# Where the head's values are split, and how they are fetched, in a two-term fp32 attention kernel

## The chip, the core and the metric

The kernel runs on one core of one Trainium2 chip. The metric is device time in microseconds of one execution, from start to end of the program, and less is better. Five engines work side by side, each through its own list of instructions in order: TensorE (PE: matmuls, with its weight loads shown as PEld), VectorE (DVE), ScalarE (ACT), GpSimd (POOL) and SyncE (SP), which here issues every DMA. They meet only at semaphores: an engine that waits holds up everything that is behind the wait in its own list.

## What is computed

One transformer layer on x of 2048 x 256, in fp32: attention with 16 heads of width 128, and a gated feed-forward part. Cut to what matters here:

```python
xn = layernorm(x)
k, q, v = (einsum('ihd,bpd->biph', W, xn) for W in (W_K, W_Q, W_V))   # 16 heads of 128
scores = einsum('biph,biqh->biqp', k, q)
masked = scores * mask - 1e10 * (1 - mask)                            # causal
attn   = softmax(masked / sqrt(128))
z      = einsum('biqp,biph->biqh', attn, v)
out    = x + einsum('df,bqf->bqd', W_O, z_flat) + ffn(xn)
```

fp32 accuracy comes from two terms: each operand is split into a part `hi` (rounded to fp32r by ACT) and a part `lo` (the rest, subtracted by DVE or POOL), and each product is three matmuls, hi·hi, hi·lo and lo·hi (`mm3`, L970 to L972).

## The kernel before

A front part (the first 250 us or so) does the layer norm, the feed-forward part and the values of all heads, which go to DRAM as `all_values`, one block of 1 MB for each head. Then come 16 heads, one after the other, in 8 steps each (`period(h)`, written once for each engine; heads 1 to 14 are a hardware loop), and a short `over` period that ends the last head.

**A step.** Step s handles two rows of 128 queries: the big row 15 - s and the small row s, 17 tiles of 128 keys together. PE makes their scores into five PSUM banks (`scores`), DVE takes the row maxima (`maxima`, L887 to L895), ACT the exponentials into the SBUF buffer `raw` (`exponential`, L655, in three pieces), and DVE transposes 32x32 blocks in place (`transpose_blocks`, L902). The rest of the transposition is done by DMA through DRAM: SP sends the row to `scratch` (`send`, L353, eight DMAs a step: four for the big row, four for the small) and brings it back into `pt_lo` (`bring`, L367, two a step). Then ACT makes `pt_hi` (`p_to_hi`, L662), POOL makes `pt_lo` (`p_to_lo`, L462), both in three pieces, and PE multiplies with the values (`weighted_sum`).

**The order of SP.** In step s: bring of step s - 1, then send of step s. A bring waits until the sends of its row have landed; the send behind it in the list waits for `blocked` (the DVE transposes of step s). `raw` holds two steps, so ACT's first exponential of step s + 2 waits until the sends of step s have landed (`stored`).

**The weighted sums.** Eight chunks z of 256 queries a head, in the order 7, 0, 6, 1, 5, 2, 4, 3 (`Z_ORDER`). Those with even z (big, `Z_BIG`) are spread over two steps, those with odd z (`Z_SMALL`) take one. Chunk z = 0 of head h is multiplied in steps 4 (keys 8 to 15, values quarters 2 and 3) and 5 (keys 0 to 7, quarters 0 and 1). Each z is split again (`z_to_hi` on ACT, L673, `z_to_lo` on DVE, L906), multiplied with W_O on PE (`output`), scaled by ACT into `share` (L682) and added by POOL (`add`, L453).

**The values of a head.** `bring_v(h)` (L372) fetches 1 MB into `v_next` in one DMA, at the end of SP's step 5 of the head before, ahead of the bring of step 5. They are split in quarters of 512 columns: `v_to_hi` on ACT (L635) and `v_to_lo` on POOL (L467), quarter 3 in step 0, quarter 2 in step 3, and quarters 0 and 1 in step 4 (`V_AT`). In step 4 ACT does them behind the exponentials, `output` and `wo_to_hi`; POOL behind `add`. `v_to_hi(h, 0)` also waits for `z_product` of z = 7 of the head before (step 3 of PE).

**Keys and queries of the next head.** Made in slices by PE in steps 0 to 7 (`project_kq`), split by ACT (`kq_to_hi`, L596) and DVE (`kq_to_lo`, L866, L869). Slice K2 is PE's last work of step 7; in ACT's list it stands behind the three `p_to_hi` of step 7, and right behind it, at the start of step 0, stands `z_to_hi` of z = 3. On DVE `z_to_lo` of z = 3 stands ahead of the maxima of step 0.

Of the kernel before, what the change touches and what calls it, by code (L numbers as in the profile page):

```python
# [12 lines left out]
BANK = 512  # L13
# [5 lines left out]
def attention_ffn_kernel(nc, x, w_heads, w_values, w1t, w3t, w2t, hadamard, out):  # L19
# [11 lines left out]
    HEADS = w_heads.shape[0]  # L31
# [3 lines left out]
    QUARTERS = S // BANK  # L35
    PER_Q = BANK // P
# [53 lines left out]

    V_ITEMS = [3, 2, 0, 1]
    V_AT = {0: [3], 3: [2], 4: [0, 1]}
    KQ_FIRST = 6

    with ExitStack() as ctx:
# [3 lines left out]
        def sem(name):  # L99
            return ctx.enter_context(nc.semaphore(name))  # L100
# [140 lines left out]
        qk_split, wo_split = sem("qk_split"), sem("wo_split")  # L241
        projected, proj_hi, proj_lo = sem("projected"), sem("proj_hi"), sem("proj_lo")
        v_projected, v_copied, v_stored = sem("v_projected"), sem("v_copied"), [sem("v_stored0"), sem("v_stored1")]
        v_moved = sem("v_moved")
        late_projected, late_copied = sem("late_projected"), sem("late_copied")
        late_stored = [sem(f"late_stored{i}") for i in range(4)]
        v_hi_done, v_lo_done, v2_read = sem("v_hi_done"), sem("v_lo_done"), sem("v2_read")
# [19 lines left out]
        def wait(engine, semaphore, count):  # L267

            if not isinstance(count, int) or count > 0:
                engine.wait_ge(semaphore, count)  # L270
# [5 lines left out]
        def v_count(h, b):  # L276
            return QUARTERS * h + V_ITEMS.index(b) + 1
# [30 lines left out]
        def _(sp):  # L308
# [57 lines left out]
                to = pt_row(pt_lo, j).bitcast(F32).rearrange("p a i q -> p a (i q)")  # L366
                sp.dma_start(to, scratch[j].rearrange("p (a x) -> p a x", a=4)).then_inc(moved[small], 16)  # L367

            def bring_v(h):

                wait(sp, v_lo_done, QUARTERS * h)
                sp.dma_start(v_next[:, :], all_values[h].rearrange("p i d -> p (i d)")).then_inc(v_moved, 16)  # L372

            for i in range(2):
                sp.wait_ge(v_stored[i], 16 * TILES // 2)
            bring_v(0)
            for h in range(HEADS):
                for s in range(STEPS):
                    if s == 0 and h + 1 < HEADS:
                        sp.wait_ge(qk_split, h + 1)  # L380
                        sp.dma_start(w_raw[:, 0:2, :], w_heads[h + 1][:, 0:2, :]).then_inc(qk_loaded, 16)
                    if s == 6 and h + 1 < HEADS:
                        sp.wait_ge(wo_split, h + 1)
                        sp.dma_start(w_raw[:, 3, :], w_heads[h + 1][:, 2, :]).then_inc(wo_loaded, 16)
                    hh, ss = step_before(h, s, 1)
                    if hh >= 0 and not on_tensor(hh, ss):
                        bring(hh, ss, 0)
                        bring(hh, ss, 1)
                    if not on_tensor(h, s):
                        send(h, s, 0)  # L390
                        send(h, s, 1)
                    if h == 0 and s < 4:
                        store_late(2 * s)
                        store_late(2 * s + 1)
                    if h == 0 and s == 5:
                        for i in range(4):
                            sp.wait_ge(late_stored[i], 16 * LATE_UNITS // 4)
                    if s == 5 and h + 1 < HEADS:
                        bring_v(h + 1)
            for z in range(CHUNKS):  # L400
                c = Z_ORDER[z]
                sp.wait_ge(out_added, z_count(HEADS - 1, z))
# [4 lines left out]
        def _(pool):  # L407
# [62 lines left out]
            def period(h, first=False, more=True, over=False):  # L470

                for s in range(5 if over else STEPS):
                    if (s - 1) in O_BIG or s == 0:
                        back, z = O_BIG[(s - 1) % STEPS]
                        if s == 0:
                            back -= 1
                        if not (first and back) and not (over and not back):
                            add(h + back, z)
                    if s == 2 and more and not over:
                        split_qk(h + 1)  # L480
                    for b in [] if over else V_AT.get(s, []):
                        v_to_lo(h, b)
                    if s == 4 and not over:
                        split_o(h)
                    hh, ss = step_before(h, s, 2)
                    if not (first and s < 2) and not over:
                        for n in range(3):
                            p_to_lo(hh, ss, n)

                    if s != 2 and s in O_SMALL or s == 3:  # L490
                        back, z = O_SMALL[2 if s == 3 else s]
                        if not (first and back) and not (over and not back):
                            add(h + back, z)
# [21 lines left out]
        def _(act):  # L515
# [76 lines left out]
            def kq_to_hi(h, item):  # L592
                which, b = item
                to = (k_hi if which == "K" else q_hi)[:, b * BANK:(b + 1) * BANK]
                act.wait_ge(projected, kq_count(h, item))
                act.activation(to, kq_bank(h, item), ACT.Copy, scale=1.0 if which == "K" else SCALE  # L596
                               ).then_inc(proj_hi, 1)
# [26 lines left out]

            def v_to_hi(h, b):
                sl = slice(b * BANK, (b + 1) * BANK)
                act.wait_ge(v_moved, 16 * h + 16)

                if b == 3:
                    wait(act, z_product, z_count(h - 1, 2))  # L630
                elif b == 2:
                    wait(act, v2_read, h)
                elif b == 0:
                    wait(act, z_product, z_count(h - 1, 7))
                act.copy(v_hi[:, sl], v_next[:, sl]).then_inc(v_hi_done, 1)  # L635
# [50 lines left out]
            def period(h, first=False, more=True, over=False):  # L686
                def absent(back):
                    return first and back or over and not back

                for s in range(5 if over else STEPS):  # L690
                    if s == 0 and not absent(O_SMALL[s][0]):
                        z_to_hi(h + O_SMALL[s][0], O_SMALL[s][1])
                    if (s - 1) in O_BIG or s == 0:
                        back, z = O_BIG[(s - 1) % STEPS]
# [1 line left out]
                            back -= 1  # L696
                        if not absent(back):
                            output(h + back, z)
                    if s == 3 and not over:
                        v_to_hi(h, 2)  # L700
                    if s in (1, 3) and not absent(O_BIG[s][0]):
                        z_to_hi(h + O_BIG[s][0], O_BIG[s][1])
                    if not over:
# [20 lines left out]
                    if s == 3 and more and not over:  # L724
                        kq_to_hi(h, ("K", 3))
                    if s >= 5 and more and not over:
                        kq_to_hi(h, (("Q", 3), ("Q", 0), ("K", 1))[s - 5])
                    for b in [] if over or s == 3 else V_AT.get(s, []):
                        v_to_hi(h, b)
                    if first and s < 4:  # L730
                        late_copy(2 * s)
                        late_copy(2 * s + 1)
# [1 line left out]
                    if over and s < 2:  # L734
                        for n in range(5):
                            transposed_to_hi(5 * s + n)
                    if not (first and s < 2) and not over:
                        p_to_hi(hh, ss, 0)
                    if s in (1, 3, 5) and not absent(Z_SMALL[s][0]):
                        z_to_hi(h + Z_SMALL[s][0], Z_SMALL[s][1])  # L740
                    if not (first and s < 2) and not over:
                        p_to_hi(hh, ss, 1)
                        p_to_hi(hh, ss, 2)
                    if s == 7 and more:
                        kq_to_hi(h, ("K", 2))

            act.activation(table_use[:, 2:3], ones[:, :], ACT.Exp)
            qk_to_hi(0)
            for i, n in V_UNITS:
# [499 lines left out]
```

## Time and profile before

| | us |
|---|---|
| median of 3 runs (lowest, highest) | 1411.65 (1407.65, 1414.73) |
| the profiled execution, its own time | 1413.05 |
| its span, first to last instruction | 1411.0 |
| PE busy in the span | 1342.5 (95%) |
| DVE, ACT, POOL busy | 938.8, 950.2, 961.2 (67%, 67%, 68%) |
| DMA traffic | 330.72 MB, mean 234 GB/s |
| mean granted TensorE clock | 0.984 |

A busy share is time in which the engine had an instruction of its own running. Waits are idle times of an engine ahead of an instruction, with what ended them. SP has no busy time: it issues DMAs, and its line in the timeline shows for how long an issue held it. One head takes some 70 us, and the rows further down are nearly all of one head, which on PE goes from 775.36 us (scores of step 3) to 845.64 us (the same point of the next head).

### The profile page before, as it was taken

The page shows a single profiled execution, that of the slowest core. Times are in us where ns is not written, and L with a number is a line of the kernel's source. Part 1 is how long each engine was busy: PE and PEld are TensorE (multiplying, and loading weights), DVE is VectorE, ACT ScalarE, POOL GpSimd, SP SyncE. Part 2 cuts the span into 40 slices and gives each one's busy share as a digit, 9 for nine tenths or more (in the row PEclk, how much of TensorE's full clock was granted, in tenths as well). Part 3 has the DMA queues.
Part 4 walks back from the last instruction along what each step waited for, and adds up shares of the span by engine and source line. Part 5 has one row for each costly group of instructions (what it writes and reads, how often), then busy time and mean ns, then how long its engine had stood idle before and what let it go on. Part 6 is the DMA issues. An engine that isn't in the chain of part 4 may idle for free.

```text
span 1411.0 us, 26546 instructions
## 1 busy us (share of the span) xinstructions
PE 1342.5 (95%) x8138; PEld 1198.1 (85%) x8138; DVE 938.8 (67%) x2131; ACT 950.2 (67%) x1926; POOL 961.2 (68%) x634
## 2 busy tenths in 40 slices
PE   6999999999999999999999999999999999999987
PEld 5788888788888888888888888888888888888876
DVE  6544200767767777777777777787777777777763
ACT  4332344677768777778776877787778777877774
POOL 6111000277869787879787978797879787978794
PEclk9999999999999999999999999999999999999999
DMA  4200166797888889888888898888898889898883
GB/s 151 71 1 0 37 193 189 205 293 252 263 271 258 287 259 288 259 285 259 281 258 270 272 283 269 286 266 287 259 286 264 287 262 290 256 287 263 278 252 98
DMA packets 275741, 330.72 MB, mean 234 GB/s; under 512 B 62576, under 2 KB 248048, under 8 KB 271344
## 3 DMA queue, kind: packets, MB, share of 16 engines
q1 hardware_dynamic: 275696, 330.19, 74.6%
q8 instruction: 20, 0.33, 0.1%
q14 instruction: 25, 0.20, 0.1%
HBM read 170.85 MB, written 159.25 MB: 234 GB/s over the span
## 4 chain that ended last, share of the span: by engine, by line
POOL 41%; issue 29%; PE 17%; DMA 4%; SPq 3%; DVE 3%; ACT 2%; POOLq 1%; ACTq 0%; DVEq 0%
POOL pt_lo L462 28%; POOL acc L453 9%; PE ps L970 6%; PE ps L971 6%; PE ps L972 6%; SPq L353 3%; DMA scratch<-raw 3%; POOL v_lo L467 3%; DMA pt_lo<-scratch 1%; POOL wqk_lo L442 1%; DVE raw L902 1%; ACT raw L655 1%; POOLq L461 1%; DVE had L892 0%; DVE pt_lo L913 0%
## 5 line engine op out<-in xcount | busy, mean ns | idle before, releaser
L462 POOL TENSOR_TENSOR pt_lo<-pt_lo,pt_hi 128x896 fp32r<-128x896 f32 (+2 forms) x378 | 651.8, 1756 | 140.1 <-ACT pt_hi L662 140.0
L655 ACT ACTIVATE raw<-ps,had 128x1024 f32<-128x1024 f32 (+7 forms) x384 | 329.4, 867 | 163.6 <-DVE had L895 133.7
L902 DVE STREAM_TRANSPOSE raw<-raw 128x2048 f32<-128x2048 f32 (+3 forms) x252 | 317.0, 1292 | 105.5 <-ACT raw L655 103.2
L970 PE MATMUL ps<-pt_hi,v_hi 128*128 128x256 f32 (+1 forms) x1152 | 327.1, 284 | 35.1 <-POOL v_lo L467 27.4
L971 PE MATMUL ps<-pt_lo,v_hi 128*128 128x256 f32 (+1 forms) x1152 | 333.2, 289 | 0.0
L972 PE MATMUL ps<-pt_hi,v_lo 128*128 128x256 f32 (+1 forms) x1152 | 331.0, 287 | 0.0
L662 ACT CAST pt_hi<-pt_lo 128x896 fp32r<-128x896 f32 (+2 forms) x378 | 284.5, 818 | 35.4 <-DMA pt_lo<-scratch 35.1
L892 DVE TENSOR_REDUCE had<-ps 128x1 f32<-128x1024 f32 (+1 forms) x256 | 237.4, 947 | 46.9 <-PE ps L972 46.7
L970 PEld LDWEIGHTS ps<-pt_hi,v_hi 128*128 128x128 f32 x1152 | 223.2, 194 | 46.0 <-POOL v_lo L467 30.6
L970 PE MATMUL ps<-k_hi,q_hi 128*128 128x512 f32 (+3 forms) x640 | 235.7, 368 | 7.0 <-DVE k_lo L866 5.9
L971 PE MATMUL ps<-k_lo,q_hi 128*128 128x512 f32 (+3 forms) x640 | 233.8, 365 | 0.0
L972 PE MATMUL ps<-k_hi,q_lo 128*128 128x512 f32 (+3 forms) x640 | 233.3, 364 | 0.0
L971 PEld LDWEIGHTS ps<-pt_lo,v_hi 128*128 128x128 f32 x1152 | 222.7, 193 | 5.5
L972 PEld LDWEIGHTS ps<-pt_hi,v_lo 128*128 128x128 f32 x1152 | 225.3, 196 | 0.0
L467 POOL TENSOR_TENSOR v_lo<-v_next,v_hi 128x512 fp32r<-128x512 f32 x64 | 82.0, 1291 | 162.9 <-ACT v_hi L635 162.9
L453 POOL TENSOR_TENSOR acc<-aux,acc 128x512 f32<-128x512 f32 x128 | 165.3, 1298 | 13.2 <-ACT aux L682 13.2
L970 PEld LDWEIGHTS ps<-k_hi,q_hi 128*128 128x128 f32 x640 | 121.3, 189 | 32.1 <-DVE k_lo L866 12.7
L972 PEld LDWEIGHTS ps<-k_hi,q_lo 128*128 128x128 f32 x640 | 121.0, 189 | 19.2
L971 PEld LDWEIGHTS ps<-k_lo,q_hi 128*128 128x128 f32 x640 | 121.4, 190 | 17.8
L887 DVE CUSTOM_DVE_ANT_0 ps<-ps,aux 128x512 f32<-128x512 f32 (+3 forms) x256 | 126.9, 496 | 0.6 <-issue 0.6
L866 DVE TENSOR_TENSOR k_lo<-ps,k_hi 128x512 fp32r<-128x512 f32 x64 | 43.1, 673 | 120.5 <-ACT k_hi L596 120.5
L682 ACT ACTIVATE aux<-ps,had 128x256 f32<-128x256 f32 x256 | 108.8, 485 | 14.0 <-issue 11.0
(113 smaller groups left out, 2222.6 us busy)
## 6 DMA issues: line engine op xcount, KB each, us to landing
v_next<-all_values SPq DMA_DIRECT2D x16, 1024.0 KB, 5.4
scratch<-raw SPq DMA_DIRECT2D x64, 256.0 KB, 5.6
pt_lo<-scratch SPq DMA_DIRECT2D x16, 1024.0 KB, 5.4
scratch<-raw SPq DMA_DIRECT2D x64, 240.0 KB, 5.0
pt_lo<-scratch SPq DMA_DIRECT2D x16, 960.0 KB, 5.9
scratch<-raw SPq DMA_DIRECT2D x64, 224.0 KB, 5.2
pt_lo<-scratch SPq DMA_DIRECT2D x16, 896.0 KB, 4.7
scratch<-raw SPq DMA_DIRECT2D x64, 208.0 KB, 4.7
```

The costliest lines, as they stand in the source:

```text
L453: pool.tensor_tensor(acc[:, 2 * c:2 * c + 2, :], share[:, z % 2, :, :], acc[:, 2 * c:2 * c + 2, :], ALU.add).then_inc(out_added, 1)
L462: pool.tensor_tensor(lo, lo.bitcast(F32), hi.bitcast(F32), ALU.subtract).then_inc(pt_lo_done, 1)
L467: pool.tensor_tensor(v_lo[:, sl], v_next[:, sl], v_hi[:, sl].bitcast(F32), ALU.subtract).then_inc(v_lo_done, 1)
L655: act.activation(to, scores, ACT.Exp, bias=neg_max[:, j:j + 1], accum_out=row_part[:, j, e % 2:e % 2 + 1]).then_inc(exped, 1)
L662: act.copy(pt_row(pt_hi, j, a, b), pt_row(pt_lo, j, a, b).bitcast(F32)).then_inc(pt_hi_done, 1)
L682: ins = act.activation(share[:, z % 2, t, :], z_bank(z, t * D, (t + 1) * D), ACT.Copy, scale=row_rcp[:, j:j + 1])
L887: dve.tensor_tensor_reduce(out=scores, in0=scores, in1=mask[:, BANK - n:], scale=1.0, scalar=-3e38, op0=ALU.add, op1=ALU.max, accum_out=ba ...
L892: dve.tensor_reduce(bank_max[:, j, i:i + 1], scores, AX_X, ALU.max).then_inc(maxed, 1)
L902: dve.transpose(v, v).then_inc(blocked, 1)
L970: pe.matmul(dst, a[0], b[0], start=start, stop=False, skip_group_check=True)
L971: pe.matmul(dst, a[0], b[1], start=False, stop=False, skip_group_check=True)
L972: return pe.matmul(dst, a[1], b[0], start=False, stop=stop, skip_group_check=True)
```

## The change

Five edits:

1. The values of the next head come in four DMAs of 256 KB, each with a semaphore of its own. Quarters 3 and 2 are issued at the end of SP's step 6, quarter 0 at the end of step 7, quarter 1 at the end of step 0 of the next head. Each waits for the `v_to_lo` of the same quarter of the head before.
2. In step 4 ACT does `v_to_hi` of quarters 0 and 1 ahead of the exponentials (behind `output` of z = 6), and POOL does `v_to_lo` of them first, ahead of `add` of z = 6.
3. ACT does `kq_to_hi` of K2 right behind that of K1, ahead of the three `p_to_hi` of step 7.
4. In the last head, which has no K1 and K2 to follow, `z_to_hi` of z = 3 moves from the `over` period into step 7, ahead of the `p_to_hi` of step 7.
5. The first quarters (head 0) are issued as four DMAs in the order 3, 2, 0, 1.

```diff
     V_AT = {0: [3], 3: [2], 4: [0, 1]}
+    V_NEXT = {6: (3, 2), 7: (0,)}
@@ SP
-            def bring_v(h):
-                wait(sp, v_lo_done, QUARTERS * h)
-                sp.dma_start(v_next[:, :], all_values[h].rearrange("p i d -> p (i d)")).then_inc(v_moved, 16)
+            def bring_v(h, b):
+                wait(sp, v_lo_done, v_count(h - 1, b))
+                sp.dma_start(v_next[:, b * BANK:(b + 1) * BANK],
+                             all_values[h][:, b * PER_Q:(b + 1) * PER_Q, :].rearrange("p i d -> p (i d)")
+                             ).then_inc(v_moved[b], 16)
-            bring_v(0)
+            for b in V_ITEMS:
+                bring_v(0, b)
...
-                    if s == 5 and h + 1 < HEADS:
-                        bring_v(h + 1)
+                    for b in V_NEXT.get(s, ()) if h + 1 < HEADS else ():
+                        bring_v(h + 1, b)
+                    if s == 0 and h > 0:
+                        bring_v(h, V_ITEMS[-1])
@@ POOL, period
                 for s in range(5 if over else STEPS):
+                    for b in V_AT[4] if s == 4 and not over else []:
+                        v_to_lo(h, b)
...
-                    for b in [] if over else V_AT.get(s, []):
+                    for b in [] if over or s == 4 else V_AT.get(s, []):
                         v_to_lo(h, b)
@@ ACT, v_to_hi and period
-                act.wait_ge(v_moved, 16 * h + 16)
+                act.wait_ge(v_moved[b], 16 * h + 16)
...
-                    if s == 0 and not absent(O_SMALL[s][0]):
+                    if s == 0 and not absent(O_SMALL[s][0]) and not over:
                         z_to_hi(h + O_SMALL[s][0], O_SMALL[s][1])
...
-                    if s == 3 and not over:
-                        v_to_hi(h, 2)
+                    for b in V_AT[s] if s in (3, 4) and not over else []:
+                        v_to_hi(h, b)
...
-                        kq_to_hi(h, (("Q", 3), ("Q", 0), ("K", 1))[s - 5])
-                    for b in [] if over or s == 3 else V_AT.get(s, []):
-                        v_to_hi(h, b)
+                        for item in ([("Q", 3)], [("Q", 0)], [("K", 1), ("K", 2)])[s - 5]:
+                            kq_to_hi(h, item)
+                    if s == 0 and not over:
+                        v_to_hi(h, V_ITEMS[0])
...
-                    if not (first and s < 2) and not over:
+                    if not (first and s < 2) and not over and not (s == 7 and not more):
                         p_to_hi(hh, ss, 0)
-                    if s in (1, 3, 5) and not absent(Z_SMALL[s][0]):
+                    if s in ((1, 3, 5) if more else Z_SMALL) and not absent(Z_SMALL[s][0]):
                         z_to_hi(h + Z_SMALL[s][0], Z_SMALL[s][1])
                     if not (first and s < 2) and not over:
+                        if s == 7 and not more:
+                            p_to_hi(hh, ss, 0)
                         p_to_hi(hh, ss, 1)
                         p_to_hi(hh, ss, 2)
-                    if s == 7 and more:
-                        kq_to_hi(h, ("K", 2))
```

## Rows read from the trace of the kernel before

**Rows 1.** Busy by engine, clock and DMA share: one head; 3.4 us at half clock.

```profile
core 0: us, PE busy (x) PEld busy (x) DVE busy (x) ACT busy (x) POOL busy (x), PEclk, DMA share, GB/s
775.36:845.64 70.28, 67.75 (x435) 61.27 (x434) 53.57 (x124) 53.52 (x111) 58.30 (x39) 1.00 0.89 277
868.09:871.50 3.41, 3.41 (x19) 3.41 (x18) 0.00 (x0) 0.34 (x2) 3.41 (x2) 0.50 1.02 349
```

**Rows 2.** Waits of PE, whole span: us in total, times, longest us.

```profile
PE ps L970 <- POOL v_lo L467: 27.4, 15, 2.4
PE ps L970 <- DVE z_lo L906: 7.6, 7, 1.9
PE ps L970 <- DVE k_lo L866: 5.9, 5, 2.7
```

**Rows 3.** Timeline of PE: start us, us, line, operation, [idle before <- what ended it].

```profile
797.50 0.39 PE L970 MATMUL ps<-pt_hi,v_hi 128*128 128x256 f32 x1 [2.33 <-POOL v_lo L467]
...
826.18 0.33 PE L970 MATMUL ps<-wo_hi,z_hi 128*128 128x256 f32 x1
```

**Rows 4.** Waits of the DMA queue (SP), 443 to 1288 us, twelve heads.

```profile
SPq L365 <- DMA scratch<-raw: 124.9, 150, 3.7
SPq L353 <- DVE raw L902: 23.9, 27, 2.0
```

**Rows 5.** Timeline of SP: the brings of steps 5 and 6, the sends of step 0.

```profile
813.36 1.19 SPq L367 DMA_DIRECT2D pt_lo<-scratch  x2
...
823.48 1.81 SPq L367 DMA_DIRECT2D pt_lo<-scratch  x2
...
833.35 6.89 SPq L353 DMA_DIRECT2D scratch<-raw  x8
```

**Rows 6.** Windows of 3 us about the brings of steps 4, 5, 6, 7, 0.

```profile
803.90:806.90 3.00, 3.00 (x20) 2.70 (x19) 2.96 (x9) 2.20 (x5) 3.00 (x3) 1.00 0.69 149
812.40:815.40 3.00, 3.00 (x19) 2.60 (x18) 1.11 (x1) 0.53 (x1) 3.00 (x3) 1.00 0.92 264
822.50:825.50 3.00, 2.96 (x14) 2.09 (x13) 1.84 (x3) 2.02 (x5) 3.00 (x3) 1.00 0.78 221
830.60:833.60 3.00, 3.00 (x17) 2.60 (x16) 3.00 (x4) 3.00 (x6) 1.70 (x2) 1.00 0.90 260
840.30:843.30 3.00, 3.00 (x18) 2.67 (x18) 3.00 (x6) 2.50 (x6) 2.91 (x3) 1.00 0.40 76
```

**Rows 7.** Timeline of ACT, steps 3 and 4.

```profile
785.68 0.94 ACT L662 CAST pt_hi<-pt_lo 128x896 fp32r<-128x896 f32 x1 [1.18 <-DMA pt_lo<-scratch]
...
789.56 1.12 ACT L655 ACTIVATE raw<-ps,had 128x1024 f32<-128x1024 f32 x1 [0.67 <-DMA scratch<-raw]
...
794.23 1.15 ACT L635 CAST v_hi<-v_next 128x512 fp32r<-128x512 f32 x2
```

**Rows 8.** Timeline of POOL, steps 3 and 4.

```profile
786.70 5.17 POOL L462 TENSOR_TENSOR pt_lo<-pt_lo,pt_hi 128x896 fp32r<-128x896 f32 x3 [1.98 <-ACT pt_hi L662]
791.83 2.55 POOL L453 TENSOR_TENSOR acc<-aux,acc 128x512 f32<-128x512 f32 x2
794.94 2.50 POOL L467 TENSOR_TENSOR v_lo<-v_next,v_hi 128x512 fp32r<-128x512 f32 x2 [0.56 <-ACT v_hi L635]
```

**Rows 9.** Timeline of ACT, end of step 7, then step 2.

```profile
820.71 2.20 ACT L662 CAST pt_hi<-pt_lo 128x896 fp32r<-128x896 f32 x3 [0.50 <-DMA pt_lo<-scratch]
823.02 0.60 ACT L596 ACTIVATE k_hi<-ps 128x512 fp32r<-128x512 f32 x1
823.52 0.37 ACT L673 CAST z_hi<-ps 128x256 fp32r<-128x256 f32 x1
...
844.19 1.12 ACT L655 ACTIVATE raw<-ps,had 128x1024 f32<-128x1024 f32 x1 [1.40 <-DVE had L895]
```

**Rows 10.** Timeline of DVE in step 0: first maxima, then the transposes.

```profile
824.59 1.81 DVE L892 TENSOR_REDUCE had<-ps 128x1 f32<-128x1024 f32 x2
...
829.78 2.50 DVE L902 STREAM_TRANSPOSE raw<-raw 128x2048 f32<-128x2048 f32 x2 [1.53 <-ACT raw L655]
```

More of the change, by code:

```diff
@@ L243, in attention_ffn_kernel @@
         v_projected, v_copied, v_stored = sem("v_projected"), sem("v_copied"), [sem("v_stored0"), sem("v_stored1")]
-        v_moved = sem("v_moved")
+        v_moved = [sem(f"v_moved{b}") for b in range(QUARTERS)]
         late_projected, late_copied = sem("late_projected"), sem("late_copied")
```

## The prediction

> **What bounds the kernel now.** I read the busy times by window first. In one head PE works 67.75 of 70.28 us, at full clock, and no other engine more than 58.30 [rows 1]. So PE looks like the bound, with 2.5 us of idle time in a head. The waits of PE name it: 27.4 us in 15 times are for `v_lo` [rows 2]. The timeline shows where, in step 5 ahead of the second half of chunk z = 0: PE stood from 795.17 to 797.50 us, until POOL had the `lo` of quarters 0 and 1 [rows 3]. Other waits are small: 5.9 us for `k_lo` in five heads, 7.6 us for `z_lo`, mostly at the two ends of the program [rows 2]. Behind a wait for `v_lo` the clock can fall to its lower level, 1.2 GHz, for 3.4 us (868.09 to 871.50, granted 0.50, 19 matmuls in it) [rows 1].
>
> But a kernel whose PE waits in each head for the same thing isn't bound by PE, and the question is what the late thing itself waited for. Going back: the `v_hi` of quarters 0 and 1 stood on ACT at 794.23, behind the exponentials of step 4, and these started at 789.56 because `raw` was free only then: "<-DMA scratch<-raw" [rows 7]. So I read the DMA queue. SP waited 124.9 us in twelve heads, 10.4 us a head, for the landing of sends before it could issue the bring behind them, and for DVE only 23.9 us, 2.0 a head [rows 4]. The sends of step 0 were issued at 833.35, while DVE had ended the transposes at 832.28, 1.07 us before [rows 5, 10]. So DMA has a closed loop of its own: sends land, the bring goes out, the next sends go out behind it. It is busy 0.89 of the head [rows 1], and idle only about each bring, since between the landing of the last send and the first data of the bring nothing is queued. Idle time in the 3 us about the bring (3 times one less the share) is 0.93 us in step 4, 0.24 in step 5, 0.66 in step 6, 0.30 in step 7 and 1.80 in step 0 [rows 6]. In steps 5 and 7 something else lies in the queue there: the 1 MB of values with w_o, and w_q and w_k.
>
> My reading is two loops of nearly one length. The DMA loop sets 70.28 us. The loop through compute (sends of step 2 land, exponentials of step 4, `v_lo`, PE from step 5 to step 0, transposes, sends of step 0) is shorter by the 1.07 us that DVE was early: 69.2 us.
>
> **The change, part by part.** *Values in quarters (edits 1 and 5).* Full DMA moves 277/0.89 = 311 GB/s here [rows 1], so 1 MB (1.05 million bytes) takes 3.37 us, a quarter 0.84. From step 5 3.37 us go; the hole about its bring comes back, from 0.24 to what step 4 has less w_o's 128 KB (0.93 - 0.42 = 0.51): saved 3.37 - 0.27 = 3.10. In step 6 two quarters come, 1.69 us, and the hole of 0.66 can shrink to 0.24: cost 1.27. In step 7 one, hole 0.30 to 0.24: 0.78. In step 0 one into a hole of 1.80: nothing. Net the DMA loop gets 3.10 - 2.05 = 1.05 us shorter. The bounds: no hole filled, 3.37 saved and 3.37 paid, 0 (I exclude a loss by this alone, since the bytes are the same and a head has 80 other DMAs, which run back to back); all holes filled to the end, 1.7. I take 1.0. On SP three issues more fall where SP waits anyway (10.4 us a head [rows 4]). The quarters are in time: quarter 1, the last, is issued about 840 and read some 20 us later, in step 4. Behind quarter 1 stands the bring of step 0, whose rows ACT reads in step 2; with a hole of 1.80 and 0.84 us of data it isn't late. The new waits of the DMAs for `v_lo` are for work of the head before, done since step 4: no cost.
>
> *Quarters 0 and 1 first in step 4 (edit 2).* POOL ended the `p_to_lo` of step 3 at 791.87, has one add of 1.27 us left from step 3, then the two `v_lo` (2.50 us): ready at 795.6 instead of 797.44 [rows 8]. ACT has the `v_hi` before that: it was free from 788.9 to 789.56, so the 1.15 us of the two delay the exponentials by 0.5 us [rows 7], which are followed by the same amount less. PE's wait falls from 2.33 to 0.5, 1.8 us in a head like this. What is next late there is POOL, whose `p_to_lo` hang on the landing of the bring of step 1 (785.68) [rows 7]. `add` of z = 6 comes 2.5 us later; nobody waits for it within a step. The clock drops should go with the wait.
>
> *K2 ahead of the three `p_to_hi` (edit 3).* This works against the rest. In the trace K2 starts at 823.02, right when PE has it, and the three pieces (2.20 us) have filled the time before [rows 9]. Afterwards ACT idles there, and the pieces come between K2 and `z_hi` of z = 3: that one ends at 826.1 instead of 823.9. On DVE the `z_lo` behind it blocks the maxima of step 0: 826.5 instead of 824.59, 1.9 us later [rows 10]. PE wants that `z_lo` at 826.18 [rows 3]: a new wait of 0.35. The transposes move by 1.9 less 1.8 from edit 2, so the compute loop stays near 69.2, with a slack of about 1 us. A second chain comes near: maxima of step 0 to the exponential of step 2, which ended at 845.31, and PE's scores of step 3 at 845.64 need its bank: 0.33 us early [rows 1, 9]. A loop through this is at most 70.28 - 2.33 + 1.9 - 0.33 = 69.5 us. For the gain side: the `k_lo` waits (5.9 us in five heads [rows 2]) come where the three pieces waited for their bring behind the 1 MB; both edits end them. In heads that DMA paces they were partly slack; of 0 to 5.9 I take 2.
>
> *Last head (edit 4).* PE's longest wait for `z_lo`, 1.9 us [rows 2], is there, where z = 3 stood behind pieces that waited for DMA. It goes; then PE wants those pieces sooner. Of 0 to 1.9 I take 1.
>
> **The sum.** The DMA loop falls to 69.3, the compute chains allow 69.2 to 69.5, PE needs 67.75 + 0.35 + 0.5. I take 0.9 us a head. Fifteen turns from head to head give 13.5, with 2 and 1 it is 16.5 us. The profiled execution took 1413.05 (span 1411.0 and 2.05 about it), 1.4 above the median: 1396.5, and about 1395 against the median.
>
> **A rule that speaks against it.** Rows first: the eight sends of a step, smaller than a quarter or as large, are issued in 6.89 us one behind the other [rows 5], and the DMA engines stand still for only 0.11 of a head [rows 1], so small DMAs cost no more than their bytes here as long as others are queued. The Trainium skill (page "DMA: Bandwidth & Descriptors", sections "Anatomy of one DMA" and "Measured") counts about 2 us for each DMA besides its bytes, and says to batch to 1 MiB or more. By it four quarters would take 10.4 us in place of 4.4, an estimate from its fit, 6 us more a head and a time near 1500. The trace agrees only where the queue runs dry.
>
> **The rivals.**
> - *DMA paces and gets nothing.* The quarters only shift the holes. Then the 1.8 us at `v_lo` turn into other waits, and 2 to 5 us are left from the `k_lo` waits and the tail: 1408. For it: the holes of steps 6 and 7 are small already [rows 6]. Chance 0.20.
> - *PE becomes the bound.* If the holes fill and both chains have more slack than I see, a head takes 67.75 + 0.35 = 68.1, 2.2 less than now: 33 + 3 us, 1376. For it: the clock drops vanish too. Against: the 0.33 us ahead of the scores of step 3. Chance 0.14.
> - *K2's place decides (slower).* If edit 2 gives less than 1.9 + 0.35 - 1.07 = 1.2 us, because POOL gets to `v_lo` late, the transposes of step 0 come later than the DMA queue can take them, and the compute loop sets the pace: 69.2 + 1.9 + 0.35 = 71.45, 1.2 us a head, 18 us less 3: 1427. The place is DVE at the start of step 0. Chance 0.10.
> - *Each quarter opens a hole.* If each of three more DMAs opens one like step 4's 0.93 us, the loop gains 1.0 and loses 2.8, 27 us in all: 1436. That is the page's rule as a mechanism of this kernel. Against: the back-to-back sends. Chance 0.03.
>
> **How the numbers follow.** Forecast 0.53: 1395, itself 1387 to 1403 (0.4 to 1.4 us a head). About 0.5% (7 us) is what can be told from no change. Faster by more: the forecast, the PE case and a little of the first rival, 0.69. Within: 0.18. Slower: 0.13. The range leaves out the two slower rivals and reaches from the PE case to the upper end of the first one: 1376 to 1411.
>
> **What would show it.** Right: PE's wait for `v_lo` at 0.5 us a head or less and hardly any stretch at 0.50; the bring of step 5 to that of step 6 down from 10.12 us [rows 5] to about 7.5, step 6 to 7 up by 1.3 and 7 to 0 by 0.8; a head near 69.3 us; new small waits of PE at `z_lo` of z = 3 and ahead of the scores of step 3; maxima of step 0 about 3.5 us behind K2. Wrong: a head still at 70.3 with the bring gaps only moved; DVE late for the sends of step 0 in most heads.

## The result, and the profile after

The changed kernel takes 1413.95 us (median of 20 runs, 1405.98 to 1420.77) and the kernel before, on the same chips, 1408.56 us (20 runs, 1402.18 to 1415.71): ratio 1.0035, 95% interval 1.0018 to 1.0052. It is 5 us slower, where I had forecast 15 us faster, and it lies above my range. The profiled execution took 1413.35 us, span 1411.3, granted clock 0.993. That of the kernel before had taken 1413.05 us, which is 4.5 us over the median of these 20 runs: the two spans that the traces show, 1411.0 and 1411.3 us, differ by less than the medians do. The busy times of the profile's page:

```profile
PE 1346.3 (95%) x8138; PEld 1192.4 (84%) x8138; DVE 939.4 (67%) x2131; ACT 950.7 (67%) x1926; POOL 960.0 (68%) x634
```

The waits of PE, and ACT's two for DMA (us in total, times, longest us):

```profile
PE ps L979 <- DVE z_lo L915: 16.2, 17, 1.8
PE ps L979 <- ACT aux L691: 9.3, 15, 0.7
PE ps L979 <- POOL v_lo L474: 5.7, 11, 0.6
PE ps L979 <- ACT raw L664: 5.2, 16, 1.4
...
ACT raw L664 <- DMA scratch<-raw: 67.7, 53, 3.1
ACT pt_hi L671 <- DMA pt_lo<-scratch: 58.5, 41, 3.1
```

The 27.4 us at `v_lo` are down to 5.7 and the waits for `k_lo` [rows 2] are gone. In their place are small waits in nearly every head, at `z_lo`, at `aux` and for `raw`. ACT's waits for DMA, 29.4 and 35.1 us in the kernel before, are now 67.7 and 58.5. PE does its work at a better clock and then waits for the same DMA loop as before. One head of PE (columns as in [rows 1]):

```profile
1145.47:1216.08 70.61, 68.70 (x433) 61.58 (x433) 53.70 (x125) 53.58 (x111) 58.24 (x39) 1.00 0.89 274
```

70.61 us at a DMA share of 0.89, as before (70.28 and 0.89 [rows 1]). So I measured the DMA loop itself: in SP's timeline the distance from the issue of the bring of step s to that of step s + 1, as a mean over all 15 turns from one head to the next. These means are worked out from the start times of those rows, from the bring of step 0 of head 0 to that of head 15. A DMA issued ahead of the bring of step s shows in the column "s", from that bring to the next.

| kernel | 0 | 1 | 2 | 3 | 4 | 5 | 6 | 7 | turn |
|---|---|---|---|---|---|---|---|---|---|
| before | 8.63 | 8.69 | 8.24 | 8.76 | 8.40 | 10.13 | 8.34 | 9.95 | 71.14 |
| after | 9.59 | 8.96 | 8.15 | 8.64 | 8.04 | 8.39 | 9.42 | 10.13 | 71.33 |
| difference | +0.96 | +0.27 | -0.09 | -0.12 | -0.36 | -1.74 | +1.08 | +0.18 | +0.19 |
| I had predicted | 0 | 0 | 0 | 0 | 0 | -3.10 | +1.27 | +0.78 | -1.05 |

Two things limit this table. Head 0 has no quarter in step 0; in heads 1 to 14 alone that column grew by 1.05 us (8.55 to 9.60). And it is one execution of each kernel: the profiled ones took from 2.5 us less (e3) to 4.5 us more (before) than the median of their kernel, -0.17 to +0.30 us a head. Fifteen times +0.19 is 2.9 us, where the medians differ by 5.4; the rest is not in these rows, and can be this scatter.

### The profile page after: what moved, and what is told of

Its sections match the earlier page's. It is cut to its first block, busy times and chain, and to the rows that moved or that the text cites. A ratio compares the mean times of both kernels' runs of the same rounds, so it can differ in the third digit from the quotient of the medians.

```text
span 1411.3 us, 26594 instructions
## 1 busy us (share of the span) xinstructions
PE 1346.3 (95%) x8138; PEld 1192.4 (84%) x8138; DVE 939.4 (67%) x2131; ACT 950.7 (67%) x1926; POOL 960.0 (68%) x634
## 4 chain that ended last, share of the span: by engine, by line
POOL 38%; issue 26%; PE 17%; DMA 6%; SPq 5%; DVE 4%; ACT 2%; POOLq 1%; ACTq 0%; DVEq 0%
POOL pt_lo L469 26%; POOL acc L460 7%; PE ps L979 6%; PE ps L980 6%; PE ps L981 6%; SPq L355 4%; DMA scratch<-raw 3%; POOL v_lo L474 3%; DVE raw L911 2%; DMA pt_lo<-scratch 2%; POOL wqk_lo L449 1%; ACT raw L664 1%; DMA acc<-x 1%; POOL wo_lo L454 1%; DVE had L901 0%
## 5 line engine op out<-in xcount | busy, mean ns | idle before, releaser
L671 ACT CAST pt_hi<-pt_lo 128x896 fp32r<-128x896 f32 (+2 forms) x378 | 283.1, 811 | 58.8 <-DMA pt_lo<-scratch 58.5
L915 DVE TENSOR_TENSOR z_lo<-ps,z_hi 128x256 fp32r<-128x256 f32 x128 | 53.9, 421 | 99.9 <-ACT z_hi L682 99.6
```

The costliest lines, as they stand in the source:

```text
L671: act.copy(pt_row(pt_hi, j, a, b), pt_row(pt_lo, j, a, b).bitcast(F32)).then_inc(pt_hi_done, 1)
```

## The experiments

The changed kernel and the 14 others that ran, with the edits that they have of the five above (1 quarters, 2 values first in step 4, 3 K2 ahead of `p_to_hi`, 4 last head, 5 quarters of head 0). Each ratio is to the kernel before, measured beside it on the same chip; the medians of different rows are from different chips and should not be compared. "Turn" and the four columns are the means defined above.

| kernel | edits | median | ratio [95%] | 5 | 6 | 7 | 0 | turn |
|---|---|---|---|---|---|---|---|---|
| after | 1 to 5 | 1413.95 | 1.0035 [1.0018, 1.0052] | 8.39 | 9.42 | 10.13 | 9.59 | 71.33 |
| e3 | 1, 5 | 1416.56 | 1.0066 [1.0045, 1.0087] | 8.38 | 9.37 | 10.15 | 9.76 | 71.38 |
| e4 | 2 | 1408.59 | 0.9997 [0.9981, 1.0013] | 10.03 | 8.37 | 9.79 | 8.52 | 70.76 |
| e5 | 3 | 1406.91 | 0.9983 [0.9968, 0.9997] | 10.21 | 8.36 | 9.72 | 8.59 | 70.78 |
| e2 | 2, 3, 4 | 1407.41 | 0.9975 [0.9958, 0.9992] | 10.00 | 8.39 | 9.71 | 8.59 | 70.82 |
| e1 | all but 3 | 1412.43 | 1.0029 [1.0015, 1.0044] | 8.50 | 9.52 | 10.05 | 9.38 | 71.36 |
| e7 | no fetch | 1383.24 | 0.9790 [0.9772, 0.9809] | 8.40 | 8.35 | 10.07 | 8.67 | 69.37 |
| e8 | four quarters in step 5 | 1421.70 | 1.0067 [1.0051, 1.0083] | 9.56 | 8.39 | 9.90 | 8.50 | 72.16 |
| e9 | e3, last one in step 7 | 1404.64 | 0.9954 [0.9939, 0.9970] | 8.49 | 9.47 | 10.50 | 8.60 | 70.79 |
| e10 | after, last one in step 7 | 1405.21 | 0.9946 [0.9922, 0.9969] | 8.45 | 9.41 | 10.50 | 8.54 | 70.84 |
| e11 | e3, last one in step 1 | 1418.21 | 1.0050 [1.0026, 1.0075] | 8.47 | 9.39 | 10.20 | 8.84 | 71.45 |
| e12 | e3, last one ahead of the sends | 1408.54 | 0.9969 [0.9948, 0.9991] | 8.45 | 9.33 | 10.71 | 8.52 | 70.92 |
| e14 | e3, last one amid the sends | 1406.97 | 0.9967 [0.9951, 0.9984] | 8.48 | 9.40 | 10.41 | 8.85 | 70.94 |
| e13 | e10 with two halves | 1404.12 | 0.9933 [0.9908, 0.9959] | 8.45 | 9.37 | 10.27 | 8.58 | 70.58 |
| e15 | e13, in steps 5 and 6 | 1406.30 | 0.9953 [0.9932, 0.9973] | 9.41 | 9.05 | 9.67 | 8.65 | 71.05 |

**The change cut in parts.** First, is it the quarters or the orders on the engines that cost? Edits 1 and 5 alone:

```diff
-                    if s == 5 and h + 1 < HEADS:
-                        bring_v(h + 1)
+                    for b in V_NEXT.get(s, ()) if h + 1 < HEADS else ():
+                        bring_v(h + 1, b)
+                    if s == 0 and h > 0:
+                        bring_v(h, V_ITEMS[-1])
```

> Only edits 1 and 5: the values in four DMAs, behind the sends of steps 6, 7 and 0. Theory A (K2's place on ACT is what eats the gain): the quarters are innocent, the DMA loop gets shorter by up to 1 us a head and the kernel is 0 to 15 us faster than before. Theory B (a quarter queued behind the sends delays the sends' landing, and with it the bring and all behind it; in the changed kernel bring of step 0 to bring of step 1 grew from 8.52 to 9.57 us): the loop of brings stays at 70.6 to 71 us a head and this kernel is by itself 2 to 6 us slower than before.

The quarters alone make it slower, by 0.66%, a little more than I had expected. Edit 2 alone:

```diff
+                    for b in V_AT[4] if s == 4 and not over else []:
+                        v_to_lo(h, b)
...
-                    if s == 3 and not over:
-                        v_to_hi(h, 2)
+                    for b in V_AT[s] if s in (3, 4) and not over else []:
+                        v_to_hi(h, b)
```

> Only edit 2: quarters 0 and 1 split first in step 4 by ACT and POOL; the values in one DMA as before. Both theories: PE's wait for v_lo falls from 27 us to some 8 us in all. If PE's chain sets the time, this is 8 to 20 us faster than before. If the DMA loop sets it (theory B), the 1.8 us a head come back as other small waits and the time is within 3 us of before.

No difference. Its waits of PE:

```profile
PE ps L973 <- DVE k_lo L869: 24.1, 16, 3.0
PE ps L973 <- DVE z_lo L909: 9.8, 8, 2.5
PE ps L973 <- POOL v_lo L469: 6.0, 12, 0.5
```

The wait left `v_lo` and went, nearly as large, to `k_lo`: PE gets to K2 earlier, and K2 on ACT stands behind pieces that wait for DMA. Edit 3 alone:

```diff
-                        kq_to_hi(h, (("Q", 3), ("Q", 0), ("K", 1))[s - 5])
+                        for item in ([("Q", 3)], [("Q", 0)], [("K", 1), ("K", 2)])[s - 5]:
+                            kq_to_hi(h, item)
...
-                    if s == 7 and more:
-                        kq_to_hi(h, ("K", 2))
```

> Only edit 3: K2's hi part ahead of the three pieces of step 7. Theory A: z_hi of z = 3 ends 2.2 us later, the maxima of step 0 start 1.9 us later, and the kernel is 5 to 18 us slower than before. Theory B: the delay is slack, since DVE is 1.1 us or more ahead of the DMA queue, and the time is within 3 us of before.

Faster by 0.17%, with 21.6 us still at `v_lo`. The changed kernel without edit 3 (the same lines the other way):

```diff
-                        for item in ([("Q", 3)], [("Q", 0)], [("K", 1), ("K", 2)])[s - 5]:
-                            kq_to_hi(h, item)
+                        kq_to_hi(h, (("Q", 3), ("Q", 0), ("K", 1))[s - 5])
...
+                    if s == 7 and more:
+                        kq_to_hi(h, ("K", 2))
```

> The changed kernel with edit 3 undone: K2's hi part again behind the three pieces. Theory A: faster than the changed kernel by 8 us or more, and faster than before. Theory B: within 3 us of the changed kernel (ratio to before 1.002 to 1.005).

1.0029 without edit 3 and 1.0035 with it, with intervals that overlap: K2's place does not decide, and that rival falls. And the changed kernel with the values as one DMA again:

```diff
-                    for b in V_NEXT.get(s, ()) if h + 1 < HEADS else ():
-                        bring_v(h + 1, b)
-                    if s == 0 and h > 0:
-                        bring_v(h, V_ITEMS[-1])
+                    if s == 5 and h + 1 < HEADS:
+                        bring_v(h + 1)
```

> The changed kernel with edits 1 and 5 undone: one DMA of 1 MB at the end of step 5, all orders on ACT and POOL as changed. Theory B (the quarters are the whole loss): 1404 to 1408 us, 0.1 to 0.4% faster than before, since the orders alone gave 0.9997 and 0.9983. Theory A (the order on ACT costs): slower than before.

0.9975. The orders on the engines give 0.25%, the quarters cost 0.66%; together 1.0041, about the 1.0035 of the whole change. All of the loss is in how the values are fetched.

**What the fetch costs at all.** The kernel before, with no values fetched for heads 1 to 15 (they use those of head 0, so the output is another one; all else is done):

```diff
-                    if s == 5 and h + 1 < HEADS:
-                        bring_v(h + 1)
...
-                act.wait_ge(v_moved, 16 * h + 16)
+                act.wait_ge(v_moved, 16)
```

> Kernel before without the fetch of values for heads 1 to 15: v_next keeps head 0's values, so the output is not the reference's; all other work is the same. If the DMA loop sets the time, the 1 MB is on its path: bring of step 5 to bring of step 6 falls from 10.1 to 8 us, and the kernel gets 15 to 35 us faster. If compute sets it, within 5 us of before.

29.6 us less (0.0210 of the 1411.68 us of the kernel before beside it), 2.0 us a head (1.77 by the table of turns). PE's wait in that kernel:

```profile
PE ps L968 <- POOL v_lo L465: 22.5, 15, 2.4
```

PE still waits for `v_lo` in 15 heads, up to 2.4 us, and each head is 2 us shorter. Most of that wait is PE's slack against the DMA loop and no cost, and the DMA loop sets the time. The run also gives the size of the prize: the 1 MB costs 2.16 us in columns 4 and 5, where I had put 3.37 us.

**Where the quarters stand.** Two readings were left. Either a DMA of 256 KB costs more than its bytes wherever it stands, or it costs where it is issued into a queue that runs dry, right ahead of a bring. First all four where the one had been (kernel before, quarters alone):

```diff
-    V_NEXT = {6: (3, 2), 7: (0,)}
+    V_NEXT = {5: (3, 2, 0, 1)}
...
-                    if s == 0 and h > 0:
-                        bring_v(h, V_ITEMS[-1])
```

> Kernel before with the values in four DMAs, all at the end of step 5 where the one was. If it is the number of DMAs and their size that cost, as slow as the quarters spread out (1.0066). If it is their place, each in another step's queue behind the sends, within 2 us of before.

1.0067. SP's timeline shows the reason, and it is neither reading:

```profile
806.60 5.41 SPq L355 DMA_DIRECT2D scratch<-raw  x8
812.05 1.87 SPq L374 DMA_DIRECT2D v_next<-all_values  x4
813.97 0.43 SPq L389 DMA_DIRECT2D w_raw<-w_heads  x1
814.49 1.18 SPq L369 DMA_DIRECT2D pt_lo<-scratch  x2
```

Four issues hold SP for 1.87 us where one held it 0.45, and the bring stands behind them. Column 4 grew from 8.40 to 9.88, about that much. So this run does not tell the readings apart. The next one does: only the quarter of step 0 moves, to step 7.

```diff
-    V_NEXT = {6: (3, 2), 7: (0,)}
+    V_NEXT = {6: (3, 2), 7: (0, 1)}
...
-                    if s == 0 and h > 0:
-                        bring_v(h, V_ITEMS[-1])
```

> Kernel before with quarters 3 and 2 at the end of step 6, 0 and 1 at the end of step 7, none in step 0. If the quarter of step 0 is what costs (bring of step 0 landed 1.2 us later, 1.16 us a head), half or more of the 9 us of the spread quarters is gone: 1409 to 1413. If each place costs alike, 1414 to 1417.

0.9954, against 1.0066 with that quarter in step 0: the same four DMAs of the same bytes, and 1.1% between them. At 1404.64 us it is faster than both of the cases that I had allowed. The same edit on the whole change:

> The changed kernel with the last quarter moved from step 0 to step 7 (3 and 2 in step 6, 0 and 1 in step 7), all orders as changed. If the quarter of step 0 is the loss and the orders are worth their 0.2 to 0.3% on top: 0.992 to 0.995 of before, the fastest so far. If the orders gain nothing once DMA is faster: 0.995 to 0.997.

0.9946 against 1.0035, 0.9%. In the table the turn is 0.5 to 0.6 us shorter for both pairs: column 0 gives back 1.05 to 1.16, column 7 takes 0.35 to 0.37. (That is 7 to 9 us in 15 turns, and the ratios say 13 to 16 us. The way is the same; the sizes agree only within the scatter of single executions.) SP's timeline of the same head shows it, first of the changed kernel:

```profile
682.96 1.43 SPq L369 DMA_DIRECT2D pt_lo<-scratch  x2
684.55 7.20 SPq L355 DMA_DIRECT2D scratch<-raw  x8
691.80 0.43 SPq L374 DMA_DIRECT2D v_next<-all_values  x1
692.61 1.19 SPq L369 DMA_DIRECT2D pt_lo<-scratch  x2
693.89 7.39 SPq L355 DMA_DIRECT2D scratch<-raw  x8
703.01 1.19 SPq L369 DMA_DIRECT2D pt_lo<-scratch  x2
```

and of e9:

```profile
682.34 1.59 SPq L369 DMA_DIRECT2D pt_lo<-scratch  x2
684.51 6.62 SPq L355 DMA_DIRECT2D scratch<-raw  x8
692.83 1.23 SPq L369 DMA_DIRECT2D pt_lo<-scratch  x2
694.15 6.89 SPq L355 DMA_DIRECT2D scratch<-raw  x8
701.72 1.19 SPq L369 DMA_DIRECT2D pt_lo<-scratch  x2
```

The quarter is issued 0.81 us ahead of the bring (691.80, 692.61), and from there to the next bring it is 10.40 us; without it 8.89. SP's waits in that stretch say which loop is late: for the landing of sends 0.40 us before and 1.28 after (0.44 in e9, 1.45 in e3), for DVE 0.11 and 0.14 (0.11, 0.21), means of heads 1 to 14. So it is DMA itself, and not compute behind a late bring. Is it step 0 or the short lead? Three kernels have the quarter in this place (after, e3, e1), 45 heads in all. In the three heads where it happened to be issued over 2 us ahead, the distance was 8.43, 8.49 and 8.58 us, as without it; in the other 42 it was 8.62 to 11.45. Among those the lead orders nothing (in e3 10.69 us at a lead of 1.84 and 8.62 at 1.05), so this is a hint and not more. One of the three, in the changed kernel:

```profile
1118.85 0.43 SPq L374 DMA_DIRECT2D v_next<-all_values  x1
1121.49 1.24 SPq L369 DMA_DIRECT2D pt_lo<-scratch  x2
1130.07 1.46 SPq L369 DMA_DIRECT2D pt_lo<-scratch  x2
```

And as an experiment, the quarter one step later, again right ahead of a bring:

```diff
-                    if s == 0 and h > 0:
+                    if s == 1 and h > 0:
                         bring_v(h, V_ITEMS[-1])
```

> Only the quarters, the last one in step 1 in place of step 0. If a third place with a DMA behind the sends costs 1 us a head wherever it is: as slow as the quarters alone (1.0066). If it is something of step 0 (the brings of 8 KB rows behind it, or DVE late there): 0.995 to 1.000.

1.0050, slow as well; column 1 is 9.66 us against 8.88 in e9. Its SP timeline, quarter and bring 0.53 us apart:

```profile
845.34 0.43 SPq L374 DMA_DIRECT2D v_next<-all_values  x1
845.87 1.19 SPq L369 DMA_DIRECT2D pt_lo<-scratch  x2
...
855.71 1.35 SPq L369 DMA_DIRECT2D pt_lo<-scratch  x2
```

Then the same step 0, but a long lead: the quarter between the bring and the eight sends,

```diff
+                    if s == 0 and h > 0:
+                        bring_v(h, V_ITEMS[-1])
                     if not on_tensor(h, s):
                         send(h, s, 0)
                         send(h, s, 1)
```

> Only the quarters, that of step 0 issued behind the brings and ahead of the sends. If what costs is that it stands right in front of the bring of step 0, which then lands 1.2 us later: that landing goes back to 5.4 us and the kernel to 0.996 to 1.000. If the bytes in step 0 cost wherever they stand in its queue: 1.004 to 1.008.

and between the four sends of the big row and the four of the small one:

```diff
                         send(h, s, 0)
+                        if s == 0 and h > 0:
+                            bring_v(h, V_ITEMS[-1])
                         send(h, s, 1)
```

> Only the quarters, that of step 0 between the four big and the four small sends. If what decides is how long ahead of the bring it is issued: bring of step 0 to bring of step 1 back to 8.5 to 8.7 us, bring landed after 5.4 us, kernel 0.996 to 0.999 of before, as with the quarter ahead of all sends (0.9969). If any data between sends and bring costs: 1.003 to 1.007.

0.9969 and 0.9967. The bring of step 0 is no longer held up. DMA issues from 443 to 1288 us (KB each, median us from issue to landing): the bring of the big row of step 0 (1024 KB) and of step 1 (960 KB), and the ones behind the other values, steps 5, 6 and 7 (704, 640, 576 KB). Before:

```profile
pt_lo<-scratch SPq DMA_DIRECT2D x12, 1024.0 KB, 5.3
pt_lo<-scratch SPq DMA_DIRECT2D x12, 960.0 KB, 5.9
...
pt_lo<-scratch SPq DMA_DIRECT2D x12, 704.0 KB, 7.1
pt_lo<-scratch SPq DMA_DIRECT2D x12, 640.0 KB, 4.2
pt_lo<-scratch SPq DMA_DIRECT2D x12, 576.0 KB, 5.4
```

After:

```profile
v_next<-all_values SPq DMA_DIRECT2D x48, 256.0 KB, 5.1
pt_lo<-scratch SPq DMA_DIRECT2D x12, 1024.0 KB, 6.8
...
pt_lo<-scratch SPq DMA_DIRECT2D x12, 704.0 KB, 5.4
pt_lo<-scratch SPq DMA_DIRECT2D x12, 640.0 KB, 6.4
pt_lo<-scratch SPq DMA_DIRECT2D x12, 576.0 KB, 5.9
```

e9, e12 and e14, one row of each:

```profile
pt_lo<-scratch SPq DMA_DIRECT2D x12, 1024.0 KB, 5.6
```

```profile
pt_lo<-scratch SPq DMA_DIRECT2D x12, 1024.0 KB, 5.4
```

```profile
pt_lo<-scratch SPq DMA_DIRECT2D x12, 1024.0 KB, 5.2
```

And e11, where it is the bring of step 1 that is late:

```profile
pt_lo<-scratch SPq DMA_DIRECT2D x12, 1024.0 KB, 5.4
pt_lo<-scratch SPq DMA_DIRECT2D x12, 960.0 KB, 6.8
```

A quarter right ahead of the bring makes it land 1.5 us later in step 0 and 0.9 in step 1. The whole 1 MB in step 5 made its bring only 1.7 us later (7.1 against 5.4), the quarter in step 7 0.5 us, and the two in step 6 2.2 us (6.4 against 4.2).

The costs follow how idle DMA is about the bring without the fetch. In e7, in windows as in [rows 6] but in 14 heads (1 us ahead of the bring's issue to 2 us behind it), the mean idle time is 0.64 us in step 5, 0.90 in step 6, 0.59 in step 7, 1.84 in step 0 and 1.67 in step 1. The 1 MB in step 5 costs 2.16 us for 3.37 us of bytes, the two quarters in step 6 1.08 for 1.69, one in step 7 0.18 and a second one there some 0.36 for 0.84 each. One in step 0 costs 0.96 to 1.16 us and one in step 1 0.78: about its bytes, with no discount. The lead alone does not do it: the first quarter of step 6 is issued only 1.5 us ahead of its bring in the mean, that of step 0 1.2. Nor do the bytes or the number of DMAs, which are the same in e3 and e9.

With a long lead the quarter is not free either: column 7, in which it is in e12 and e14, is 10.71 and 10.41 against 10.15 in e3, and column 0 of e14 keeps 0.25 of its loss (8.85 against 8.60 in e9). That is about half of the 1.16 us of column 0, and these two kernels are 0.3% faster than before, where e9 is 0.5% faster (the intervals overlap). Last, fewer DMAs in the good places, 512 KB each (quarters 2 and 3 in step 6, 0 and 1 in step 7; the edit is shown against e10):

```diff
-    V_NEXT = {6: (3, 2), 7: (0, 1)}
+    V_NEXT = {6: (2,), 7: (0,)}
...
-                sp.dma_start(v_next[:, b * BANK:(b + 1) * BANK],
+                sp.dma_start(v_next[:, b * BANK:(b + 2) * BANK],
```

> As the changed kernel, but two DMAs of 512 KB: values 3 and 2 in step 6, 0 and 1 in step 7. Against the same with quarters it has two DMAs less and rows of 4 KB. If the number of DMAs or their row length costs (four in one place were 0.9% slower than one): 0.2 to 0.5% faster than with quarters; if not, within 2 us.

0.9933, the fastest of all, though its interval (0.9908 to 0.9959) overlaps that of e10, and its median is 1.1 us below: within the 2 us that I had named for no effect. Part of its lead over the kernel before is the orders on the engines, which gave 0.9975 by themselves (e2). And one step earlier each:

```diff
-    V_NEXT = {6: (2,), 7: (0,)}
+    V_NEXT = {5: (2,), 6: (0,)}
```

> As the two halves of 512 KB in steps 6 and 7 (0.9933 of before), but in steps 5 and 6. In both places the queue is backed up behind the sends. If only that matters: 0.992 to 0.996. If the queue's fullness in each step matters (w_o in step 5, w_q and w_k in step 7): different by 0.2% or more.

0.9953, 0.2% from e13 with intervals that overlap, which decides nothing. A half in step 5 costs 0.96 us of the 1.74 that the whole cost there (column 5: 9.41, with 8.45 without and 10.13 with all of it).

## Why the prediction was wrong

**What was right.** That the DMA loop sets the time and not the wait that PE shows: e7 takes 29.6 us less with 22.5 of the 27.4 us of wait for `v_lo` still there, and e4 ends most of that wait and gains nothing. The effects on the engines came out as written. PE's wait for `v_lo` is 0.51 us (I said 0.5):

```profile
1145.47 0.39 PE L979 MATMUL ps<-pt_hi,v_hi 128*128 128x256 f32 x1 [0.51 <-POOL v_lo L474]
...
1194.67 0.50 PE L979 MATMUL ps<-k_hi,q_hi 128*128 128x512 f32 x1 [0.24 <-ACT raw L664]
```

The second row is the new small wait ahead of the scores of step 3. K2, the pieces and the maxima behind them, ACT first:

```profile
1171.03 0.60 ACT L605 ACTIVATE k_hi<-ps 128x512 fp32r<-128x512 f32 x1 [2.82 <-PE ps L981]
1171.52 2.18 ACT L671 CAST pt_hi<-pt_lo 128x896 fp32r<-128x896 f32 x3
```

```profile
1174.01 0.42 DVE L915 TENSOR_TENSOR z_lo<-ps,z_hi 128x256 fp32r<-128x256 f32 x1 [1.66 <-ACT z_hi L682]
1174.35 1.81 DVE L901 TENSOR_REDUCE had<-ps 128x1 f32<-128x1024 f32 x2
```

ACT idles 2.82 us ahead of K2, and the maxima start 3.32 us behind it (1174.35 less 1171.03), where it was 1.57 [rows 9, 10]: 1.75 later, I had said 1.9. With edit 3 alone (e5) DVE is late for the sends of step 0: SP waits over 0.2 us between the bring of step 7 and these sends in 11 of 14 heads, 0.66 us in the mean where it was 0.18, and the kernel is not slower. With edit 2 beside it, in the changed kernel, it is 4 of 14 heads. The mean granted clock rose from 0.984 to 0.993, since fewer stretches are at the lower level, as I had said, and brought no time, since PE then waits for DMA. The end of the program gained 0.6 us (from the last bring of step 0 on, 78.2 to 77.6), where I had taken 1. Of the two signs that I had named for being wrong, the first came: a head of 70.61 us with the gaps between brings only moved.

**Edit 1, step 0: "one into a hole of 1.80: nothing".** Two terms of the sum failed, this one and that of step 5, about 1 us a head each. This is the one that turned the sign: without that quarter the kernel is faster than before (e9, e10). Measured it is +0.96 in the change, 1.05 to 1.16 against e10 and e9, some 15 us in 15 turns, and at least the 0.84 us of its bytes. The 1.80 us was idle time taken as free room. It is a mean over 16 DMA engines [rows 6], and it lies where SP waits for the sends to land and the bring has yet to start moving. The quarter was issued 0.5 to 2.6 us ahead of the bring, in most heads under 1.4, and no quarter of this kernel landed sooner than 3.4 us after its issue, so that it was still on its way when the bring went out. The windows about the bring of step 0 in the head shown above, after:

```profile
690.50:693.50 3.00, 3.00 (x18) 2.63 (x18) 3.00 (x5) 3.00 (x7) 2.72 (x3) 1.00 0.73 208
692.60:695.60 3.00, 2.99 (x22) 2.70 (x21) 3.00 (x8) 2.09 (x4) 3.00 (x3) 1.00 0.82 150
```

and e9:

```profile
690.90:693.90 3.00, 3.00 (x21) 2.70 (x21) 3.00 (x4) 3.00 (x8) 2.19 (x2) 1.00 0.52 135
692.80:695.80 3.00, 3.00 (x20) 2.71 (x19) 3.00 (x8) 2.36 (x5) 3.00 (x3) 1.00 0.58 188
```

The hole does get filled (share 0.73 for 0.52), as I had wanted, and the loop is longer for it: in the 3 us behind the bring the engines are busier, 0.82 for 0.58, and move less, 150 for 188 GB/s. The means of heads 1 to 14 say the same with less contrast: 0.77 and 174 GB/s against 0.64 and 186, and in step 1 0.73 and 124 in e11 against 0.57 and 141 in e9.

**Edit 1, step 5: 3.10 back.** Columns 4 and 5 gave 2.10. I had priced the 1 MB by its bytes (3.37 us) with 0.27 for the hole; e7 shows that it cost 2.16 there. Of the difference the hole about the bring explains 0.30 (idle time as above, 14 heads: 0.64 in e7, 0.34 before), which I had right; where the rest went no run shows. A part of the 2.10 is not DMA time at all: 0.36 is in column 4, ahead of the bring of step 5, where one issue less holds SP (0.45 us). This costs 1.0 us a head, 15 us in all: what step 5 had to give was a third less than I took it for.

**Steps 6 and 7.** +1.08 for 1.27, and +0.18 for 0.78: here I was too pessimistic, by 0.19 and 0.60. Of the others, column 1 took 0.27 and columns 2 and 3 gave 0.21. The sum: -1.05 + 0.96 + 1.00 - 0.19 - 0.60 + 0.06 = +0.18, the measured +0.19 but for rounding.

**The bounds.** I had excluded a loss "since the bytes are the same and a head has 80 other DMAs, which run back to back". That reason holds for the sends, issued behind one another into a busy queue, and says nothing of a DMA that is issued when the queue is about to run dry. It put the lower bound of the gain at 0 where it should have been below. The upper bound of 1.7 does not follow from my rows either: all holes filled gives 3.10 less 1.03 and 0.54, 1.5. The forecast also started from a median of 3 runs, 1411.65 us, that is 3.1 us above the one of 20.

**The rivals.** "DMA paces and gets nothing" (0.20) named the mechanism: PE's waits turned into others and 2 to 5 us stayed from the orders on the engines (e2: 3.5). It lacked the loss. "Each quarter opens a hole" (0.03) had the sign and the wrong extent: 1436 for every quarter, where one quarter out of four does it and two halves or four quarters in good places gain. The rule behind it, in the Trainium skill (page "DMA: Bandwidth & Descriptors", section "Anatomy of one DMA"), counts about 2 us for each DMA besides its bytes, for DMAs that GpSimd issues; here SP issues them. The traces agree for the time of one DMA in a queue run dry (the bring of step 0 before, 1024 KB, landed 5.3 us after its issue, 1.9 us more than its bytes at my 311 GB/s), and not for what a DMA costs the one behind it: a quarter in step 0 delays its bring by 1.5 us, of which by my 0.84 for the bytes 0.7 is left, and in step 7 by 0.5 us in all. "PE becomes the bound" and "K2's place decides" fell with the turn of 71.33 us and with e1.

**What stays open.** Why a quarter costs all of its bytes in steps 0 and 1. The bring of step 0 lands 1.2 to 1.6 us later with the quarter ahead of it (6.8 against 5.6, 5.4 and 5.2 in e9, e12 and e14). The lower rate behind the bring suggests that both transfers slow each other, but no run separates that from the order in the queue. What the runs show is where the loss is and how to be rid of it, and not its mechanism in the queue. Whether e13 beats e10 isn't settled either (0.9933 and 0.9946).

## What to carry to other kernels

Where DMA runs in a closed loop (send, wait for the landing, bring), a wait of a compute engine may be slack, and a run without the suspected traffic tells; taking 21 us of it away gave nothing here (e4). The idle share ahead of a dependent DMA was latency and not room in this kernel: a DMA put there cost about its bytes or more, one put where the queue was busy about the bring cost a third less or better. Price a transfer by how much later the next DMA of the loop goes out, from a run with and one without it, and not by its bytes; how late the DMA behind it lands is no measure either (2.2 us for the two quarters of step 6, which cost 1.08). And count the issues that stand between a landed transfer and the next one of the loop.

## What the runs showed of the hardware that I had not expected

- 256 KB took 5.1 us from issue to landing and 1 MB 5.5 us (medians of 48 and 12). The bring behind it landed later by 0.5 us (256 KB, step 7) to 1.5 (256 KB, step 0), by 2.2 for two of 256 KB (step 6) and by 1.7 for 1 MB (step 5).
- Each of these DMAs holds SP for about 0.45 us, and four issues ahead of a bring held it for 1.87 us: column 4 of e8 is 1.48 us longer, and its turn 72.16 us against 71.14.
- A higher DMA share came with a lower rate: 0.77 and 174 GB/s with the quarter against 0.64 and 186 without it, means of 14 windows of 3 us behind the bring of step 0.
- PE waited 28.7 us for `v_lo` in e9, which is 0.5% faster than the kernel before, and 6.0 us in e4, which is no faster.
